# Two stages of a graph-attention layer in one block, with node weights, first inputs and one low part moved

## What is computed

```python
h = jnp.maximum(_layernorm(x, axis=-1), 0.0)
# attention over the edges: scores, softmax by destination, msg = V[src] * w
out = jnp.zeros((n, H, D), msg.dtype).at[dst].add(msg)
out = out.reshape(n, OUT_DIM) @ Wo_w + Wo_b
out = _layernorm(residual + out, ln1_g, ln1_b)      # residual = h
ffn = jax.nn.gelu(out @ ffn_w1 + ffn_b1, approximate=False) @ ffn_w2 + ffn_b2
out = _layernorm(out + ffn, ln2_g, ln2_b)
x = x + out
```

## Time and profile before

| | |
|---|---|
| median of 3 runs | 1871.33 us (1869.89 to 1872.53) |
| profiled execution | 1869.43 us, span of its instructions 1867.7 us |
| tensor engine busy | 1684.7 us (90%) |
| vector engine busy | 1471.2 us (79%) |
| scores and softmax | to about 406 us of the span |
| messages | about 406 to 578 us |
| nodes | from 578 us to the end |

### The profile page before, as it was taken

One profiled execution on the slowest core, in us unless ns is written; L12 is line 12 of the kernel. 1 busy time (PEld: TensorE's weight loads), 2 busy tenths in 40 slices (PEclk: granted clock), 3 DMA queues, 4 the chain that ended last, 5 costly groups with the idle time before them and its releaser, 6 DMA issues.

```text
span 1867.7 us, 29784 instructions
## 1 busy us (share of the span) xinstructions
PE 1684.7 (90%) x9846; PEld 1411.2 (76%) x9846; DVE 1471.2 (79%) x4479; ACT 1288.1 (69%) x2340; POOL 1337.4 (72%) x1342
## 2 busy tenths in 40 slices
PE   0999999639961599999999999999999999999997
PEld 0677777418741488888888888888888888888887
DVE  3565665367732599999999999999999999999996
ACT  1677777302210688888888888888888888888884
POOL 7777774007772777877887787778778877877783
PEclk9999999859985799999999999999999999999999
DMA  3778887313434577777776777777777767776761
GB/s 104 238 258 267 267 262 221 122 57 97 136 105 148 106 167 170 168 170 170 165 172 167 175 158 174 167 170 168 169 170 167 171 166 174 158 175 166 172 132 57
DMA packets 132414, 309.41 MB, mean 166 GB/s; under 512 B 14022, under 2 KB 68214, under 8 KB 132260
## 3 DMA queue, kind: packets, MB, share of 16 engines
q0 software_dynamic: 42624, 139.33, 37.2%
q1 hardware_dynamic: 37492, 115.61, 18.3%
q10 hardware_dynamic: 52144, 52.56, 8.5%
HBM read 140.66 MB, written 118.20 MB: 139 GB/s over the span
## 4 chain that ended last, share of the span: by engine, by line
PE 66%; DMA 1%; DVE 1%; POOL 0%; ACT 0%; SPq 0%; issue 0%; DVEq 0%; POOLq 0%; ACTq 0%
PE d_F L991 30%; PE d_Y L1002 30%; PE d_T L978 5%; DMA d_fb_row<-in_fb 1%; DMA d_z<-agg_scratch 0%; PE d_Y L968 0%; ACT d_zn L903 0%; PE d_F L961 0%; SPq L727 0%; POOL d_zx_rstd L788 0%; POOL d_u L775 0%; POOL d_u L773 0%; ACT d_z L914 0%; DVE d_y_stats L847 0%; DVE d_zx_stats L860 0%
## 5 line engine op out<-in xcount | busy, mean ns | idle before, releaser
L1002 PE MATMUL d_Y<-d_w_hi,d_act_hi 128*128 128x256 f32 x1568 | 458.5, 292 | 0.0
L1002 PE MATMUL d_Y<-d_w_hi,d_act_lo 128*128 128x256 f32 x1568 | 441.8, 282 | 0.0
L1002 PE MATMUL d_Y<-d_w_lo,d_act_hi 128*128 128x256 f32 x1568 | 441.7, 282 | 0.0
L903 ACT ACTIVATE d_zn<-d_z,d_zx_nmr,d_zx_rstd 128x256 f32<-128x256 f32 x392 | 224.3, 596 | 149.1 <-POOL d_zx_nmr L791 149.1
L991 PE MATMUL d_F<-d_zt_hi,d_w_hi 128*128 128x512 f32 x784 | 321.5, 410 | 2.1 <-DVE d_zt_lo L823 1.4
L991 PE MATMUL d_F<-d_zt_hi,d_w_lo 128*128 128x512 f32 x784 | 310.2, 396 | 0.0
L991 PE MATMUL d_F<-d_zt_lo,d_w_hi 128*128 128x512 f32 x784 | 310.0, 395 | 0.0
L923 ACT ACTIVATE d_F<-d_F,d_fb_col 128x512 f32<-128x512 f32 x392 | 259.5, 662 | 61.5 <-PE d_F L991 61.4
L773 POOL TENSOR_TENSOR d_u<-d_zn,d_g_row 128x1024 f32<-128x1024 f32 x98 | 293.5, 2995 | 6.0 <-ACT d_zn L903 6.0
L1002 PEld LDWEIGHTS d_Y<-d_w_hi,d_act_lo 128*128 128x128 f32 x1568 | 296.1, 189 | 0.0
L1002 PEld LDWEIGHTS d_Y<-d_w_lo,d_act_hi 128*128 128x128 f32 x1568 | 295.9, 189 | 0.0
(11 more groups left out here) (159 smaller groups left out, 3538.5 us busy)
## 6 DMA issues: line engine op xcount, KB each, us to landing
agg_scratch<-a_bias_row ACTq DMA_DIRECT2D x50, 1024.0 KB, 6.7
d_x<-in_x SPq DMA_DIRECT2D x98, 512.0 KB, 4.1
d_z<-agg_scratch POOLq DMA_DIRECT2D x98, 512.0 KB, 5.6
d_x<-d_b_wide POOLq DMA_DIRECT2D x98, 512.0 KB, 7.5
out<-d_o SPq DMA_DIRECT2D x98, 512.0 KB, 2.9
c_cont<-cont_scratch SPq DMA_DIRECT2D x25, 256.0 KB, 3.4
a_xd<-in_x,a_idx POOLq DMA_INDIRECT x100, 2.8
a_xs<-in_x,a_idx POOLq DMA_INDIRECT x100, 4.7
```

The lines of the kernel that those rows point to most:

```text
L903: ins = nc.scalar.activation(zn[gz % 2][:, j, :], z[gz % ZR][:, j, :], ACT.Identity, bias=zx_nmr[:, at % NR, 0, j:j + 1], scale=zx_rstd[:, ...
L1002: ins = nc.tensor.matmul(Y[s % 2][:, j, :], a[:, c, j * P:(j + 1) * P], w[:, c, :], start=False, stop=(c == KF - 1 and w is w2_lo), skip_g ...
```

## The change

The last two stages become one block, `message_node_stage`; the meeting of engines between them is gone. In the rows of the new code a tile that lies in `vt` bears the name vt, and the banks of T and F bear the name low_banks.

- **Places.** `vt` is used up from the front during the messages. The raw node weights, x, z, zn, u and o lie in it. The first six x tiles are loaded as places come free.
- **SP** issues the seven loads of vectors ahead of the first `c_alpha_in`; the two weight loads, six loads of x and the wide bias follow between later groups.
- **DVE** splits the weights after groups 6 to 11, takes the statistics of x tiles 0 to 3 after groups 13 to 16, and finishes their 1/std with ACT's square root after groups 17 and 18.
- **ACT** makes h of tiles 0 to 3 after groups 19 to 22, and then one small gelu, which has its table loaded.
- **PE** makes the bias after the last message and then 48 matmuls (HEAT) whose result nobody reads. The eight that marked the banks are gone.
- **POOL** goes from the last scatter's wait straight to the node loop, which starts at step -3 instead of -6. The DMA that adds the bias to x is issued one step later.
- **In each node step** DVE makes `act_lo` of c = 0 after two of the four centrings, not after all four. ACT makes `act_hi` of c = 0 before the third normalisation of z, not after it.

```diff
+        FIRST, LAST = -3, NG + 1
+        PREP = 8
+        HEAT = 48
...
+                for to, of in vectors:
+                    sp.dma_start(to[:], of).then_inc(w_in, 16)
+                for c in range(-3, EG):
                     step(Step(c))
+                    if c == 4:
+                        sp.wait_ge(msg_done, KD * 4)
+                        sp.dma_start(w1_raw, w1.rearrange("(k p) n -> p k n", p=P)).then_inc(w_in, 16)
+                        sp.dma_start(w2_raw, w2.rearrange("(k p) n -> p k n", p=P)).then_inc(w_in, 16)
+                    if c in X_FREE:
+                        g = X_FREE.index(c)
+                        sp.wait_ge(msg_done, KD * c)
+                        sp.dma_start(xt[g], rows_of(x, g)).then_inc(x_in[g], 16)
+                    if c == 16:
+                        sp.wait_ge(msg_done, KD * 16)
+                        sp.dma_start(b2_wide, b2_of).then_inc(b2_row_in, 16)
...
+                        done(nc.vector.tensor_tensor(res_row[:], res_row[:], fb2_row[:], ALU.add))
+
+                def early_statistics(g):
+                    dve.wait_ge(x_in[g], 16)
+                    for j in range(GT):
+                        nc.vector.bn_stats(e_stats[:, g, j, :], xt[g][:, j, :]).then_inc(estats_done, 1)
+                    for j in range(GT):
+                        dve.wait_ge(estats_done, GT * g + j + 1)
+                        nc.vector.bn_aggr(e_mv[:, g, j, :], e_stats[:, g, j, :]).then_inc(emv_done, 1)
...
+                for c in range(0, EG):
+                    step(Step(c))
+                    if 6 <= c < 12:
+                        weights(c - 6)
+                    if 13 <= c < 13 + XE:
+                        early_statistics(c - 13)
+                    if c == 13 + XE:
+                        dve.wait_ge(emv_done, XE * GT)
+                        nc.vector.tensor_scalar(e_veps[:], e_mv[:, :, :, 1], LN_EPS, None, ALU.add).then_inc(e_veps_done, 1)
+                    if c == 13 + XE + 1:
+                        early_root()
...
+                    centre((0, 1))
+                    low_part(s, 0)
+                    centre((2, 3))
...
+                    if g == 13 + XE:
+                        act.wait_ge(e_veps_done, 1)
+                        nc.scalar.activation(e_std[:], e_veps[:], ACT.Sqrt).then_inc(e_std_done, 1)
+                    if 13 + XE + 2 <= g < 13 + 2 * XE + 2:
+                        early = g - 13 - XE - 2
+                        act.wait_ge(e_root, 5)
+                        for j in range(GT):
+                            ins = nc.scalar.activation(z[early][:, j, :], xt[early][:, j, :], ACT.Relu,
+                                                       bias=e_nmr[:, early, j:j + 1], scale=e_rstd[:, early, j:j + 1])
+                        ins.then_inc(h_done, 1)
+                nc.scalar.activation(gelu_ready[:], e_rstd[:, 0, 0:1], ACT.Gelu)
+                act.wait_ge(prep_d, PREP)
...
+                    norm_z((0, 1))
+                    gelu(0)
+                    high_part(0)
+                    norm_z((2,))
+                    gelu(1)
+                    norm_z((3,))
...
+                for r in range(4):
+                    pool.wait_ge(scattered[r], 16 * GT * ((EG + 3 - r) // 4))
+                pool.wait_ge(prep_d, PREP)
+                pool.wait_ge(b2_row_in, 16)
...
+                    g = s + 3
+                    if there(g):
+                        pool.wait_ge(h_done, g + 1)
+                        pool.dma_start(z[g % ZR], rows_of(agg_dram, g), accum_op=ALU.add).then_inc(agg_in[g % ZR], 16)
+                    g = s + 2
+                    if there(g):
+                        pool.dma_start(xt[g % XR], b2_wide, accum_op=ALU.add).then_inc(b2_in[g % XR], 16)
```

More of the change, by code:

```diff
@@ L477, in _, with message_node_stage @@
                 sp.wait_ge(stored, 48)
-def message_stage(nc, dst_cols, next_cols, wo, wo_b, vt, alpha_dram, cont_dram, agg_dram):
+def message_node_stage(nc, dst_cols, next_cols, wo, wo_b, vt, alpha_dram, cont_dram, agg_dram, x, given, w1, w2, out):
     with ExitStack() as ctx:
@@ L511, in message_stage, with place, rows_at @@
         WARM = 4
-        FIRST = -3
+        XR, ZR, NR, FB = 8, 4, 4, 3
+        XE = 4
+        X_FREE = (5, 6, 7, 9, 11, 13)
+        flat = vt[:].rearrange("p k e -> p (k e)")
+        def place(at, tiles=1):
+            return flat[:, at * GT * D:(at + tiles) * GT * D]
+        def rows_at(at):
+            return place(at).rearrange("p (j d) -> p j d", j=GT)
+        w1_raw, w1_scaled = place(0).rearrange("p (k n) -> p k n", k=KD), place(2).rearrange("p (k n) -> p k n", k=KD)
+        w2_raw = place(1).rearrange("p (k n) -> p k n", k=KF)
@@ new lines, in message_node_stage, with sb_first @@
+        zx_stats, zx_mv = sb("d_zx_stats", [P, NR, 2, GT, 6]), sb("d_zx_mv", [P, NR, 2, GT, 2])
+        zx_nmean, zx_veps = sb("d_zx_nmean", [P, NR, 2, GT]), sb("d_zx_veps", [P, NR, 2, GT])
+        zx_rstd, zx_nmr = sb("d_zx_rstd", [P, NR, 2, GT]), sb("d_zx_nmr", [P, NR, 2, GT])
+        y_stats, y_mv = sb("d_y_stats", [P, 2, GT, 6]), sb("d_y_mv", [P, 2, GT, 2])
+        y_veps, y_rstd = sb("d_y_veps", [P, 2, GT]), sb("d_y_rstd", [P, 2, GT])
+        with ExitStack() as first:
+            def sb_first(name, shape, dt=f32):
+                return first.enter_context(nc.sbuf_tensor(name, shape, dt))
+            msg = [sb_first(f"c_msg{r}", [P, KD, GR]) for r in range(2)]
+            total = [sb_first(f"c_total{r}", [P, KD, GR]) for r in range(2)]
+            rows = [sb_first(f"c_rows{r}", [P, GT, D]) for r in range(4)]
@@ L513, in message_stage, with there, late, wide @@
+        HEAT = 48
+        def there(g):
+            return 0 <= g < NG
+        def late(g):
+            return XE <= g < NG
+        def wide(row):
+            return row[:].rearrange("p (j d) -> p j d", j=1).broadcast_to([P, GT, D])
+        def rows_of(table, g):
+            at = g * GR if g < NG - 1 else N - GR
+            return table[bass.ds(at, GR), :].rearrange("(p j) d -> p j d", j=GT)
         with nc.Block() as block:
@@ L963, in _ @@
                 ins.then_inc(bias_ps, 1)
-                pe.wait_ge(consts, 3)
-                pe.wait_ge(prep, PREP)
-                for r in range(2):
-                    for j in range(0, GT, 2):
-                        ins = nc.tensor.matmul(Y[r][:, j:j + 2, :], ident[:], w2_raw[:, j:j + 2, :], start=True, stop=True)
-                ins.then_inc(y_open, 1)
+                pe.wait_ge(d_consts, 3)
+                pe.wait_ge(prep_d, PREP)
+                for n in range(HEAT):
+                    nc.tensor.matmul(FF[:, 2, :], w1_hi[:, 0, 0:P], w1_hi[:, n % KD, :], start=True, stop=True)
                 def transposes(g, k):
```

704 lines of the change are left out of this document (334 added, 370 removed).

## The result

The changed kernel takes 1846.38 us (median of 4 runs, 1845.73 to 1847.09), the kernel before 1870.87. The ratio is 0.9869, with a 95% interval of 0.9854 to 0.9884. The forecast was 1852, the range 1822 to 1866. The profiled execution had 1847.09 us, the span is 1845.4 us.

A forecast was written before the change was run, and what follows sets the result against it. The node step was taken to be bound by DVE's list from the finished Y to `zt_lo`, with a long hole before the nodes. From the median, 1871.3 - 37 (start) + 18 (steps) = 1852 us, range 1822 to 1866.

The forecast's parts named there:

- The hole: Between the last scatter and the first sum into z: loads, weight split and first h move earlier, 40.1 us less.
- The way from the sum's issue to the first finished Y: Start of the nodes: 2 us less before the first zn, 1 less from the gelu's table load and high part.
- The return: Cost in the messages: 4 us for SP's earlier loads, 2 for DVE's extra work; start as a whole 37 less.
- 15% of all of that work: During the messages: some 15 us of extra DVE work slows POOL's scatter issues by 15% of it, 2 us.
- The step: Each node step: DVE waits 0.19 us for act_hi before act_lo of c = 0; over 96 tiles 18 us more.
- HEAT: PE after the messages: 48 matmuls take 11.5 us, or twice that at the low clock; no cost and no gain.
- The cover that I named: First zn comes some 10 us after the last scatter lands, hiding HEAT; without it HEAT would cost up to 12.
- B: Node step: act_hi is there in time, the step stays at 12.53, time 1834 us; chance 0.17.
- C: Node step: F's wait for act_lo counts and goes, 15 us less, time 1819 us; chance 0.10.
- D: Node step: POOL gets slower, its list 1.0 us longer delays the first gelu, time 1892 us; chance 0.08.

The follow-up runs named there:

- Experiment 5: The changed kernel with SP's seven vector loads issued after group 3's loads: 1853.19 us, ratio 0.9838; run once more, 1842.93 us, ratio 0.9854.
- experiment 1: The kernel before with only the two moves inside the node step (act_lo and act_hi of c = 0), without the merged block: 1887.93 us, ratio 1.0092.
- experiment 6: The kernel before with PE's tiles moved in SBUF, three kernels; the last moved only the split weights and small statistics tiles: 1866.53 us, ratio 0.9979.
- experiment 2: The changed kernel with the old order inside the node step put back on DVE and ACT: 1830.05 us, ratio 0.9779.
- experiment 7: The changed kernel without the 48 unread matmuls (HEAT = 0): 1847.80 us, ratio 0.9883.
- experiment 3: The changed kernel with act_lo of c = 0 after three of four centrings, not two: 1828.43 us, ratio 0.9774.

## Why the prediction was right

The forecast was 5.6 us above the median. By its own steps:

**The hole.** Forecast 40.1; measured 42.79 - 2.41 = 40.4. The way from the sum's issue to the first finished Y was to be 3 shorter; it is 34.58 - 30.99 = 3.6 shorter: 2.2 between the sum's arrival and the first `zn` (forecast 2) and 1.3 behind that (forecast 1), where the table load has gone to 558.24.

**The return.** The last scatter is issued at 575.29, 7.80 later than before, where the forecast said 574. Of this 1.08 had come by the stage's first load (407.28, before 406.20) and is drift of the front, 4.5 came before the first scatter (431.40, before 425.81; forecast 4) and 2.2 in the messages (forecast 2). The sum, 40.4 + 3.6 - 7.8 = 36.2, met the forecast of 37. Experiment 5 shows SP's vectors to be 3.7 of the 4.5; for the other 0.8 no run has a cause.

That 2.2 met 2 is in part luck. From the first scatter to the last pass 143.9 us, before 141.7; but experiment 1 and the last kernel of experiment 6, whose messages are those of before, took 143.1 and 143.6. Against the mean of these three the extra is about 1 us, and no run took DVE's extra work away. Nor did it come as 15% of all of that work. In the changed kernel the five issues beside the casts, the subtractions and the addition of the split took 3.2 us more than 0.98 each, those beside the statistics took none, and all other issues together took 1.0 less than before.

**The step.** The wait was reckoned at 0.19 from three distances; it is 0.21 by the slot and 0.19 in the list (8.47 against 8.28). The mechanism is shown by experiments 1 and 2, which put the order into one kernel and take it out of the other. From the first to the last finished Y that makes 1230.9 - 1213.1 = 17.8 and 1226.9 - 1209.2 = 17.7, where the forecast said 18. What the sum lacked is a term: the steps as a whole cost 13.8, since the merged block gives 3.9 back. From `zt_lo` to the next statistics pass 4.21, no longer 4.25, and experiment 6 gets the same out of the kernel before by the place of the split weights in SBUF. The prediction has no such term, and nothing in the trace of before pointed to it. Of the 5.6 us 4.2 are the steps and 1.9 the basis (the sum was counted from the median, 1.9 above the profiled execution), against 0.8 at the start; the remaining 0.3 is rounding and the distance of the new profiled run from its median.

**HEAT** at nothing: right, by experiment 7. The cover that I named was there.

**The rivals.** B (`act_hi` in time) fell with the first trace, since the high part was ready 0.18 after the slot. C (F's wait counts) fell with experiments 1 and 3. D (POOL slower) did not come: the multiplication for `u` took 2948 ns in the mean, before 2995, and POOL waited for DVE's statistics of Y in every step.

## What to carry to other kernels

Where two engines form a loop, name the one list of instructions that closes it, and ask of each edit only what it does to that list. The larger wait in a table (29.9 us against 11.6) was the worthless one, and taking it away with moves that made the list's owner wait 0.2 us cost 17 us. When work is moved to an earlier stage, keep its loads behind the first loads of the stage that receives it, and look for the next cheap entry of the list that closes the loop: here it was one aggregation, worth 23 us.

## What the runs showed of the hardware

**Where weights lie in SBUF changes the pace of matmuls.** 128x256 matmuls with a new stationary tile each follow one another 0.119 us apart with the streamed `w2` at byte 32896 of the partitions, and 0.117 with it at 163616; `w1` and the small tiles of statistics moved along. The F matmuls of 512 columns, which load `w1` as their stationary tile, showed no difference (395 ns at both places).

**A POOL issue that begins during some DVE instructions is lengthened by what is left of them.** An indirect issue takes 0.98 us. One that begins just after the start of a scan, or with the subtraction of the weight split, which reads two tiles of SBUF, takes 1.90 to 2.05; one that begins with a cast, 1.51; one that begins with a scaling of the split, with the statistics of x, or shortly before a scan ends, 0.98. POOL and DVE in the changed kernel:

```profile
450.47 1.90 POOL L1020 DMA_INDIRECT agg_scratch<-c_rows,c_row_of  x1 [0.30 <-issue]
452.68 0.98 POOL L1020 DMA_INDIRECT agg_scratch<-c_rows,c_row_of  x1 [0.30 <-issue]
...
462.25 2.05 POOL L1020 DMA_INDIRECT agg_scratch<-c_rows,c_row_of  x1 [0.30 <-issue]
...
503.91 0.98 POOL L1020 DMA_INDIRECT agg_scratch<-c_rows,c_row_of  x1 [0.30 <-issue]
```

```profile
450.31 2.45 DVE L763 TENSOR_TENSOR_SCAN c_total<-c_cont,c_total,c_msg 128x512 f32<-128x512 f32 x2
452.68 1.23 DVE L776 TENSOR_SCALAR vt<-vt,d_g_col 128x512 f32<-128x512 f32 x2
...
462.25 1.20 DVE L780 TENSOR_TENSOR d_w_lo<-vt,d_w_hi 128x1024 fp32r<-128x1024 f32 x1
...
503.90 1.37 DVE L791 BATCH_NORM_STATS2 d_e_stats<-vt 128x6 f32<-128x256 f32 x4
```
